# Output projection in fp16 high and low parts: an attention and recurrence kernel with a hand-written order of eight steps

## Chip, cores and metric

The kernel runs on one core of one Trainium2 chip. The metric is the device time of one execution in microseconds (us), taken as the median of the runs.

## The reference

A batch of 32 sequences x (256 positions, 128 features) goes through an attention block and then through a gated recurrence over the batch index:

```python
h = rms_norm(_layernorm(x), norm_weight)            # eps 1e-5 and float32 eps
q, k, v = split(h @ w_qkv.T)                        # 16 heads of 64; rotary embedding on q and k
k, v = concat(persist_mem, k), concat(persist_mem, v)   # 4 more keys and values per head
scores = where(causal, einsum(q, k) * 64**-0.5, min)
out = einsum(softmax(scores), v)                    # 256 x 1024 per sequence
x = x + out @ w_out.T                               # 1024 -> 128: the output projection
xn = _layernorm(x)                                  # scan over the 32 sequences, state c is 256 x 128 here
ft, it = sigmoid(xt @ wf.T + c @ uf.T + bf), sigmoid(xt @ wi.T + c @ ui.T + bi)
gt = tanh(xt @ wc.T + c @ uc.T + bc)
c = ft * c + it * gt                                # after the last step:
x = x + tanh(xn @ wo.T + c_final @ uo.T + bo)
```

All inputs and the output are float32.

## The kernel before

A software pipeline runs over `j`, the number of the sequence that enters. In iteration `j` the kernel projects q and k of sequence `j`, does the softmax and the value product of `j - 1`, normalises and projects out `j - 2` (called `cj`), and takes the recurrence one sequence on with `j - 3` (`dj`). Each iteration has eight steps, `s` = 0 to 7, one per pair of heads. Every engine has a `body(j, p)` that writes out its own instructions step by step, in a fixed order; semaphores tie the engines together. There is no scheduler: what stands ahead in an engine's `body` runs ahead.

What a step holds, and its names: `project` (TensorE, q and k of one pair, three fp16 products of high and low parts), `rotate` (VectorE, the two products of the rotary embedding, which read the projection's bank), `swap` (two DMAs from SyncE's queue that exchange neighbouring rows of `rope_b` into `rope_c`), `rope_add` (GpSimd, `rope_a + rope_c` into `qk`), `hi` (ScalarE, the fp16 copy `qk_h`), `scores_for_max` (TensorE, fp16 scores into `bank_sm`), `maxima` (VectorE), `scores_t` (TensorE, the exact scores of `j - 1` into `bank_st`), `exp` (ScalarE), `prob_add` (GpSimd), `attend` (TensorE, into `bank_pv`), `raw_copy` (ScalarE, `bank_pv` into `raw`). `sums` collects the softmax denominators in `bank_sum`; `transpose_top` turns the maxima, and `copy_top` (ScalarE) copies them back for the next scores.

The output projection of `cj` goes through these functions. `invert` (VectorE, step 1) makes 1/l; `store_linv` and `spread_linv` (SyncE's queue, step 2) bring it to DRAM and from there, repeated over partitions, into `rinv` by four DMAs. `divide` (VectorE) multiplies `raw` by `rinv` in place, quarter by quarter `n` = 0 to 3: 0 and 1 in step 4, 2 and 3 in step 5. `project_out` (TensorE) multiplies a quarter of `raw` by `wo_sb` in float32, two quarters in step 5 and two in step 6, right after `project`. `residual` and `second_stats` (VectorE, step 6), `rstd` (GpSimd, step 7) and `second_norm` (ScalarE, step 7) make the input of the recurrence, `transpose_xn`, `xt_high`, `xt_low`, `gates`, `gate_tanh` and `state` take it on in the next iteration:

```python
if s in (5, 6) and c and j != NB:
    project_out(j - 2, p, 2 * (s - 5))
    project_out(j - 2, p, 2 * (s - 5) + 1)
```

## Time and profile before

| what | value |
|---|---|
| median of 3 runs | 1133.06 us (1131.0 to 1133.95) |
| the profiled execution | 1133.03 us, of which the span from first to last instruction is 1131.2 us |
| TensorE matmul busy | 1080.3 us, 95% of the span |
| VectorE, ScalarE, GpSimd busy | 930.0, 698.4, 634.8 us (82, 62, 56%) |
| mean granted TensorE clock | 0.988 of full speed |

The span is what the trace covers; 1.8 us lie around it. The profiled execution and the median agree within 0.03 us. Busy shares are means over the whole span; in the steady part the pipeline repeats every iteration, so a stretch of one iteration is what to look at.

### The profile page before, as it was taken

The numbers are of one execution on the slowest core, as the hardware profiler recorded it, in microseconds if no ns is written. First come the engines' busy times: TensorE is split into PE (matmuls) and PEld (weight loads), VectorE is DVE, ScalarE is ACT, GpSimd is POOL, SyncE is SP. The second block draws the span as 40 slices with busy tenths as digits, with TensorE's granted clock in tenths as the row PEclk, the third lists the DMA queues.
The fourth block names the chain that finished last, engine by engine and source line by source line (L and its number), as shares of the span: only waits on it lengthen the run. The fifth ranks groups of instructions, "written<-read, shape, count | busy, mean of one in ns | idle before, by whom it ended". The sixth has DMA issues, their size and how long they took to land.

```text
span 1131.2 us, 47261 instructions
## 1 busy us (share of the span) xinstructions
PE 1080.3 (95%) x18443; PEld 813.6 (72%) x18443; DVE 930.0 (82%) x3305; ACT 698.4 (62%) x1575; POOL 634.8 (56%) x816
## 2 busy tenths in 40 slices
PE   3879999999999999999999999999999999999996
PEld 2457777777777776777777777677777777777784
DVE  5778888888888888888888888788888888888745
ACT  3556666666666666666666666666665666666644
POOL 3545665576565647656555665555565565556420
PEclk8889999999999999999999999999999999999999
DMA  6213343332333442233333233333323333332215
GB/s 204 95 62 112 111 115 114 115 95 89 111 111 114 115 114 90 90 111 115 115 115 115 83 100 115 107 114 115 115 78 98 114 115 111 108 112 92 68 36 150
DMA packets 78031, 120.52 MB, mean 107 GB/s; under 512 B 13041, under 2 KB 35954, under 8 KB 77682
## 3 DMA queue, kind: packets, MB, share of 16 engines
q1 hardware_dynamic: 68714, 111.20, 32.5%
q10 hardware_dynamic: 9096, 6.30, 2.1%
q8 instruction: 147, 2.41, 1.0%
q14 instruction: 74, 0.61, 0.2%
HBM read 41.56 MB, written 8.78 MB: 45 GB/s over the span
## 4 chain that ended last, share of the span: by engine, by line
PE 59%; DVE 16%; DMA 14%; SPq 4%; issue 3%; POOL 2%; ACT 1%; DVEq 0%; POOLq 0%
PE bank_pv L1142 11%; PE bank L1034 11%; DMA rope_c<-rope_b 10%; PE bank_st L1098 8%; PE bank_sum L1179 5%; PE bank_sum L1163 4%; DVE masked L809 4%; PE bank_sm L1073 4%; PE bank L1056 3%; DMA linv_scratch<-linv 3%; SPq L312 3%; DVE linv L832 2%; DVE rope_a L798 2%; PE bank L1281 2%; PE bank L1283 2%
## 5 line engine op out<-in xcount | busy, mean ns | idle before, releaser
L407 POOL TENSOR_TENSOR qk<-rope_a,rope_c 128x512 f32<-128x512 f32 x256 | 341.0, 1332 | 312.9 <-DMA rope_c<-rope_b 288.9
L809 DVE CUSTOM_DVE_ANT_0 masked<-bank_sm,mask_q 128x132 bf16<-128x132 f32 (+1 forms) x1024 | 307.1, 355 | 17.7 <-PE bank_sm L1073 17.2
L798 DVE TENSOR_TENSOR rope_a<-bank,cos 128x512 f32<-128x512 f32 x256 | 174.1, 680 | 130.1 <-PE bank L1034 83.7
L400 POOL TENSOR_TENSOR prob<-prob 128x264 f32<-128x264 f32 x256 | 210.8, 823 | 117.1 <-ACT prob L544 108.3
L529 ACT ACTIVATE qk_h<-qk 128x512 f16<-128x512 f32 x256 | 160.4, 627 | 172.2 <-POOL qk L407 171.7
L544 ACT ACTIVATE prob<-bank_st 128x784 f32<-128x784 f32 x256 | 209.3, 817 | 59.7 <-PE bank_st L1107 58.9
L1142 PE MATMUL bank_pv<-prob,v_sb 128*64 128x256 f32 (+1 forms) x2048 | 224.8, 340 | 0.6 <-DVE raw L825 0.6
L1098 PE MATMUL bank_st<-qk 64*64 64x256 f32 (+3 forms) x4096 | 186.3, 299 | 0.4 <-issue 0.2
L1098 PEld LDWEIGHTS bank_st<-qk 64*64 64x64 f32 x4096 | 167.7, 134 | 9.6 <-issue 1.3
L799 DVE TENSOR_TENSOR rope_b<-bank,sin 128x512 f32<-128x512 f32 x256 | 173.8, 679 | 0.0
L1142 PEld LDWEIGHTS bank_pv<-prob,v_sb 128*64 128x64 f32 x2048 | 124.3, 136 | 54.4 <-issue 0.9
L1034 PE MATMUL bank<-h_hi,w_hi 128*128 128x256 f16 x512 | 143.5, 280 | 5.8 <-DVE rope_b L799 5.0
L1034 PE MATMUL bank<-h_hi,w_lo 128*128 128x256 f16 x512 | 141.8, 277 | 0.0
L1034 PE MATMUL bank<-h_lo,w_hi 128*128 128x256 f16 x512 | 141.6, 277 | 0.0
L1179 PE MATMUL bank_sum<-wo_sb,raw 128*128 128x128 f32 x992 | 122.7, 276 | 0.0
L1179 PEld LDWEIGHTS bank_sum<-wo_sb,raw 128*128 128x128 f32 x992 | 116.0, 192 | 1.9 <-DVE raw L845 1.1
L578 ACT ACTIVATE v_sb<-bank 128x512 f32<-128x512 f32 x128 | 75.8, 593 | 48.2 <-PE bank L1053 28.7
L569 ACT ACTIVATE raw<-bank_pv 128x256 f32<-128x256 f32 x256 | 97.7, 382 | 4.1 <-PE bank_pv L1148 3.1
L845 DVE SCALAR_TENSOR_TENSOR raw<-rinv,raw 128x512 f32<-128x512 f32 x124 | 96.6, 819 | 2.0 <-DMA rinv<-linv_scratch 1.8
L1073 PEld LDWEIGHTS bank_sm<-qk_h 64*64 64x64 f16 x2048 | 37.6, 105 | 82.7 <-issue 56.6
L1073 PE MATMUL bank_sm<-qk_h 64*64 64x68 f16 (+3 forms) x2048 | 86.7, 246 | 4.4 <-ACT qk_h L529 3.1
L809 DVE DVE_READ_ACCUMULATOR2_ANT top<- 128x1 bf16 x1024 | 85.7, 84 | 0.1
(237 smaller groups left out, 1732.1 us busy)
## 6 DMA issues: line engine op xcount, KB each, us to landing
rope_c<-rope_b SPq DMA_DIRECT2D x512, 128.0 KB, 2.3
rinv<-linv_scratch SPq DMA_DIRECT2D x124, 256.0 KB, 4.8
out<-x_sb SPq DMA_DIRECT2D x16, 256.0 KB, 3.7
linv_scratch<-linv SPq DMA_DIRECT2D x62, 64.0 KB, 2.1
x_sb<-x ACTq DMA_DIRECT2D x28, 128.0 KB, 5.5
xt<-w_qkv_t ACTq DMA_DIRECT2D x1, 1024.0 KB, 5.3
v_end<-v_end_scratch SPq DMA_DIRECT2D x64, 8.0 KB
v_sb<-pm_v SPq DMA_DIRECT2D x63, 8.0 KB
```

The lines of the kernel that those rows point to most:

```text
L400: G.tensor_tensor(prob_2[:, s % 4, :, :], prob[:, s % 4, :, 0:NT - Q1], prob[:, s % 4, :, C0 + Q1:SCOL], ALU.add).then_inc(S["prob_added"], 1)
L407: G.tensor_tensor(qk[:, s, :].rearrange("p (u n) -> p u n", u=2)[:, :, 0:NT], rope_a[:, (NPAIR * j + s) % 3, :].rearrange("p (u n) -> p u ...
L529: A.activation(qk_h[:, s, :].rearrange("p (u n) -> p u n", u=2)[:, :, 0:NT], qk[:, s, :].rearrange("p (u n) -> p u n", u=2)[:, :, 0:NT], A ...
L544: A.activation(prob[:, s % 4, :, :], ps_st[:, :, 0:SCOL], ACT.Exp).then_inc(S["exp_done"], 1)
L798: V.tensor_tensor(rope_a[:, (NPAIR * j + s) % 3, :], proj_bank(j, s)[:, :], cos[:, :], ALU.mult)
L799: V.tensor_tensor(rope_b[:, s % 2, :], proj_bank(j, s)[:, :], sin[:, :], ALU.mult).then_inc(S["qk_read"], 1)
L809: ins = V.tensor_tensor_reduce(masked[:, e, c0:c0 + n], ps_sm[:, e, c0:c0 + n], mask_q[:, c0:c0 + n], 1.0, LOWEST, ALU.add, ALU.max, top[: ...
L1034: last = T.matmul(proj_bank(j, s)[:, u * NT:(u + 1) * NT], W[q][:, col:col + P], H[p][:, par, NPM:NKEY], start=(i == 0), stop=(i == 2))
L1073: last = T.matmul(ps_sm[OWN[SIDE[qb]], e, c0:c0 + n], qk_h[OWN[e], s, qb * HB:qb * HB + HB], qk_h[OWN[e], s, NT:NT + n], start=True, stop= ...
L1098: T.matmul(ps_st[OWN[SIDE[kb]], e, st_cols(blk)], qk[OWN[e], s, NT + kb * HB:NT + kb * HB + HB], qk[OWN[e], s, q0:NT], start=(kc == 0), st ...
L1142: last = T.matmul(ps_pv[OWN[e], q0:NT], v_sb[:, kc, col:col + DH], prob[:, s % 4, e, c0:c0 + NT - q0], start=(kc == 0), stop=(kc == 1))
L1179: last = T.matmul(y_out(cj)[:, q * D:(q + 1) * D], raw[:, par, s, q * P:(q + 1) * P], wo_sb[:, s, :], start=(alone and s == 0 and q == 0), ...
```

## The change: what it does

- The weights of the output projection are kept as two fp16 tiles, `wo_hi` and `wo_lo` (scaled by 64), made once near the start by one ScalarE and one VectorE instruction.
- After `divide` each quarter of `raw` gets a high part, a fp16 copy (`y_high`, ScalarE, steps 4 and 5), and a low part, the rest (`y_low`, GpSimd, steps 4 and 5). `project_out` makes three fp16 products (high by high, high by low, low by high) where it made one float32 product. Both parts live in `y_hl`, whose memory is also `rinv`.
- `project_out` of quarters 0 and 1 moves to the front of step 6, that of quarters 2 and 3 to the end of step 6. `residual` and `second_stats` move to step 7, `second_norm` to step 0 of the next iteration, with `transpose_xn` and `gates` at the ends of steps 0 to 2, and the other work of the recurrence a step later.
- `spread_linv` issues its four DMAs in two halves, after `swap` of step 2 and of step 3.
- `state` has four parts in place of three: its first two operations stand apart, in steps 2 and 3.
- For the last sequence the low parts are made on VectorE (`y_low_last`).

```diff
         f_lo = sb("f_lo", [P, 8, P], f16)
-        wo_sb = sb("wo_sb", [P, NPAIR, D], f32)
+        wo_hi = sb("wo_hi", [P, NPAIR, D], f16)
+        wo_lo = sb("wo_lo", [P, NPAIR, D], f16)
...
-        rinv = sb("rinv", [P, NPAIR, NT], f32)
+        y_hl = sb("y_hl", [P, 4, 2, 2 * NT], f16)
+        rinv = y_hl[:, :, :, :].rearrange("p n u m -> p (n u m)").bitcast(f32).rearrange("p (s n) -> p s n", s=NPAIR)
...
-            def spread_linv(cj):
+            def spread_linv(cj, half):
...
                 sp.wait_ge(S["linv_stored"], 32 * (cj + 1))
                 sp.sem_inc(S["sp_tick"], 1)
-                wait(sp, S["norm_done"], 4 * cj)
+                wait(sp, S["y_ready"], cj)
                 sp.sem_inc(S["sp_tick"], 1)
-                for half in range(2):
-                    for e in range(2):
-                        src = linv_dram[e:e + 1, 2 * half:2 * half + 2, :, :].rearrange("o k b n -> o (k b n)")
-                        sp.dma_start(rinv[OWN[e], 4 * half:4 * half + 4, :].rearrange("p s n -> p (s n)"),
-                                     src.to_broadcast([64, 4 * NT])).then_inc(spread[half], 16)
+                for e in range(2):
+                    src = linv_dram[e:e + 1, 2 * half:2 * half + 2, :, :].rearrange("o k b n -> o (k b n)")
+                    sp.dma_start(rinv[OWN[e], 4 * half:4 * half + 4, :].rearrange("p s n -> p (s n)"),
+                                 src.to_broadcast([64, 4 * NT])).then_inc(spread[half], 16)
...
-                    if c and s == 2 and j - 2 < NB - 1:
-                        spread_linv(j - 2)
+                    if c and s in (2, 3) and j - 2 < NB - 1:
+                        spread_linv(j - 2, s - 2)
...
+            def y_low(cj, par, n):
+
+                pool.wait_ge(S["y_hi_done"], 4 * cj + n + 1)
+                G.tensor_tensor(y_hl[:, n, 1, :].rearrange("p (s n) -> p s n", s=2), raw[:, par, 2 * n:2 * n + 2, :],
+                                y_hl[:, n, 0, :].rearrange("p (s n) -> p s n", s=2), ALU.subtract).then_inc(S["y_lo_done"], 1)
...
-                    if c and s == 7 and j < NB:
-                        rstd(j - 2)
...
                     if s >= 1 and a:
                         rope_add(j, s - 1)
+                    if s == 4 and c and j < NB:
+                        y_low(j - 2, p, 0)
+                        y_low(j - 2, p, 1)
+                    if s == 7 and c and j < NB:
+                        rstd(j - 2)
                     if b:
                         prob_add(j - 1, s)
+                    if s == 5 and c and j < NB:
+                        y_low(j - 2, p, 2)
+                        y_low(j - 2, p, 3)
+                    if s in (5, 6) and j == NB:
+                        y_low(j - 2, p, 2 * (s - 5))
+                        y_low(j - 2, p, 2 * (s - 5) + 1)
...
+            def y_high(cj, par, n):
+
+                act.wait_ge(S["norm_done"], 4 * cj + n + 1)
+                A.activation(y_hl[:, n, 0, :].rearrange("p (s n) -> p s n", s=2), raw[:, par, 2 * n:2 * n + 2, :],
+                             ACT.Copy).then_inc(S["y_hi_done"], 1)
...
-                    if s == 3 and b:
-                        copy_top(j - 1, 1)
...
-                    if s == 0 and d and j != NB + 1:
+                    if s == (0 if j > NB else 1) and d and j != NB + 1:
                         xt_high(j - 3)
...
                         gate_tanh_last(j - 3)
-                    elif s in (1, 2) and d and j - 3 < NB - 1:
-                        gate_tanh(j - 3, s - 1)
+                    elif s in (2, 3) and d and j - 3 < NB - 1:
+                        gate_tanh(j - 3, s - 2)
+                    if s == 3 and b:
+                        copy_top(j - 1, 1)
...
-                    if s == 7 and c and j < NB:
-                        second_norm(j - 2)
+                    if s == 0 and d and j <= NB:
+                        second_norm(j - 3)
...
                     if s >= 1 and b:
                         raw_copy(j - 1, 1 - p, s - 1)
+                    if s in (4, 5) and c and j <= NB:
+                        y_high(j - 2, p, 2 * (s - 4))
+                        y_high(j - 2, p, 2 * (s - 4) + 1)
...
+                V.scalar_tensor_tensor(wo_lo[:, :, :].rearrange("p c d -> p (c d)"), o_raw, WS,
+                                       wo_hi[:, :, :].rearrange("p c d -> p (c d)"), ALU.mult,
+                                       ALU.subtract).then_inc(S["casts_dve"], 1)
...
+            def y_low_last(cj, par, n):
+
+                dve.wait_ge(S["y_hi_done"], 4 * cj + n + 1)
+                V.tensor_tensor(y_hl[:, n, 1, :].rearrange("p (s n) -> p s n", s=2), raw[:, par, 2 * n:2 * n + 2, :],
+                                y_hl[:, n, 0, :].rearrange("p (s n) -> p s n", s=2), ALU.subtract).then_inc(S["y_lo_done"], 1)
...
                 dve.wait_ge(S["y_ready"], cj + 1)
-                V.tensor_tensor(at3(x_sb, cj), y_out(cj), at3(x_sb, cj), ALU.add).then_inc(S["x1_done"], 1)
+                V.scalar_tensor_tensor(at3(x_sb, cj), y_out(cj), 1.0 / WS, at3(x_sb, cj), ALU.mult,
+                                       ALU.add).then_inc(S["x1_done"], 1)
...
-                        dve.wait_ge(S["gate_read"], 2 * dj + 2)
+                        dve.wait_ge(S["gate_read"], 2 * dj + 1)
+                    wait(dve, S["dve_s"], 3 * dj)
                     V.scalar_tensor_tensor(ga[:, :], th[:, 0, :], 1.0, c2[:, :], ALU.add, ALU.mult).then_inc(S["dve_s"], 1)
-                    if dj == NB - 1:
-                        dve.wait_ge(S["gate_read"], 2 * dj + 2)
+                elif part == 1:
+                    dve.wait_ge(S["gate_read"], 2 * dj + 2)
                     V.scalar_tensor_tensor(gb[:, :], th[:, 1, :], 1.0, th[:, 2, :], ALU.add, ALU.mult).then_inc(S["dve_s"], 1)
-                elif part == 1:
+                elif part == 2:
                     dve.wait_ge(S["dve_s"], 3 * dj + 2)
                     V.scalar_tensor_tensor(c2[:, :], ga[:, :], 0.5, gb[:, :], ALU.mult, ALU.add).then_inc(S["dve_s"], 1)
...
+                    if s == 7 and c and j < NB:
+                        residual(j - 2)
+                    if s == 1 and c:
+                        end_add(j - 2, p)
                     if a:
                         rotate(j, s)
-                    if s == 1 and c:
-                        end_add(j - 2, p)
-                    if s == 0 and d and j != NB + 1:
+                    if s == (0 if j > NB else 1) and d and j != NB + 1:
                         xt_low(j - 3)
...
+                    if s == 2 and d and j != NB + 1:
+                        state(j - 3, 0)
                     if s == 3 and d and j != NB + 1:
-                        state(j - 3, 0)
+                        state(j - 3, 1)
+                        state(j - 3, 2)
...
                     if s == 4 and c and j - 2 < NB - 1:
                         divide(j - 2, p, 0)
                         divide(j - 2, p, 1)
-                    if s == 4 and d and j != NB + 1:
-                        state(j - 3, 1)
...
+                    if s == (6 if j >= NB else 7) and c:
                         second_stats(j - 2)
...
                     if s == 6 and d and j < NB:
-                        state(j - 3, 2)
+                        state(j - 3, 3)
...
-                pe.wait_ge(S["norm_done"], 4 * cj + n + 1)
+                pe.wait_ge(S["y_lo_done"], 4 * cj + n + 1)
+                if cj == 0 and n == 0:
+                    pe.wait_ge(S["casts_dve"], 7)
                 alone = cj >= NB - 2
                 for s in (2 * n, 2 * n + 1):
                     for q in range(QT):
-                        last = T.matmul(y_out(cj)[:, q * D:(q + 1) * D], raw[:, par, s, q * P:(q + 1) * P], wo_sb[:, s, :],
-                                        start=(alone and s == 0 and q == 0), stop=(s == NPAIR - 1 and q == QT - 1),
-                                        skip_group_check=True)
+                        at = s % 2 * NT + q * P
+                        for i, (u, v) in enumerate(SPLIT):
+                            last = T.matmul(y_out(cj)[:, q * D:(q + 1) * D], y_hl[:, n, u, at:at + P], WO[v][:, s, :],
+                                            start=(alone and s == 0 and q == 0 and i == 0),
+                                            stop=(s == NPAIR - 1 and q == QT - 1 and i == 2), skip_group_check=True)
                 if n == 3:
                     last.then_inc(S["y_ready"], 1)
...
-                    elif s == 0 and d and j <= NB:
-                        transpose_xn(j, j - 3)
-                    if s in (1, 2) and d and j <= NB:
-                        gates(j, j - 3, s - 1)
...
-                    if s in (5, 6) and c and j != NB:
+                    if s == 6 and c and j < NB:
+                        project_out(j - 2, p, 0)
+                        project_out(j - 2, p, 1)
...
+                    if s == 6 and c and j < NB:
+                        project_out(j - 2, p, 2)
+                        project_out(j - 2, p, 3)
                     if s in (2, 4, 7) and b:
                         sums(j - 1, (2, 4, 7).index(s))
-                if isinstance(j, int) and j == 2:
-                    pe.wait_ge(S["casts_dve"], 6)
+                    if s == 0 and d and j <= NB:
+                        transpose_xn(j, j - 3)
+                    if s in (1, 2) and d and j <= NB:
+                        gates(j, j - 3, s - 1)
```

In these listings a row is an instruction with its source line, operation, output<-inputs and shape; "x2" stands for two in a row. GpSimd, steps 4 and 5 of an iteration with all stages active, before:

```order
L407 TENSOR_TENSOR qk<-rope_a,rope_c 128x2x256
L400 TENSOR_TENSOR prob<-prob 128x264
L407 TENSOR_TENSOR qk<-rope_a,rope_c 128x2x256
L400 TENSOR_TENSOR prob<-prob 128x264
L407 TENSOR_TENSOR qk<-rope_a,rope_c 128x2x256
```

and now (L408 is `rope_add`, L401 `prob_add`, L416 `y_low`):

```order
L408 TENSOR_TENSOR qk<-rope_a,rope_c 128x2x256
L416 TENSOR_TENSOR y_hl<-raw,y_hl 128x512 x2
L401 TENSOR_TENSOR prob<-prob 128x264
L408 TENSOR_TENSOR qk<-rope_a,rope_c 128x2x256
L401 TENSOR_TENSOR prob<-prob 128x264
L416 TENSOR_TENSOR y_hl<-raw,y_hl 128x512 x2
L408 TENSOR_TENSOR qk<-rope_a,rope_c 128x2x256
```

Between the first `rope_add` of the listing and the last, four instructions over 128x512 were put, two ahead of the `prob_add` of step 4 and two behind that of step 5.

ScalarE, steps 4 and 5, now (L597 `value_copy`, L563 `exp`, L588 `raw_copy`, L655 `y_high`, L548 `hi`, L496 `h_high`); before, the two rows of L655 were not there and the rest stood in the same order:

```order
L597 ACTIVATE v_sb<-bank 128x512
L561 ACTIVATE prob_end<-bank_st 16x2x16
L563 ACTIVATE prob<-bank_st 128x784
L588 ACTIVATE raw<-bank_pv 128x256
L655 ACTIVATE y_hl<-raw 128x512 x2
L548 ACTIVATE qk_h<-qk 128x2x256
L496 ACTIVATE h_hi<-bank,nw 128x256
L563 ACTIVATE prob<-bank_st 128x784
L588 ACTIVATE raw<-bank_pv 128x256
L655 ACTIVATE y_hl<-raw 128x512 x2
L548 ACTIVATE qk_h<-qk 128x2x256
```

The high parts stand ahead of the fp16 copy of q and k (`hi`) of the same step.

TensorE, end of step 6 now, between the last `attend` (L1191) and `transpose_top` of step 7 (L1131), the first rows of the 24 small fp16 products of quarters 2 and 3:

```order
L1191 MATMUL bank_pv<-prob,v_sb 64x132 x2
L1232 MATMUL bank_sum<-wo_hi,y_hl 128x128
L1232 MATMUL bank_sum<-wo_lo,y_hl 128x128
L1232 MATMUL bank_sum<-wo_hi,y_hl 128x128 x2
L1232 MATMUL bank_sum<-wo_lo,y_hl 128x128
```

and before, where step 6 passed from `attend` straight to `transpose_top`, and its float32 block stood behind `project`:

```order
L1034 MATMUL bank<-h_lo,w_hi 128x256
L1179 MATMUL bank_sum<-wo_sb,raw 128x128 x8
L1053 MATMUL bank<-w_hi,h_hi 128x512
```

A block of 8 float32 products became 24 fp16 products, and the second block of an iteration moved behind the rest of step 6.

## Rows read from the trace of the kernel before

**Rows 1.** The page: busy time and share of each engine

```profile
PE 1080.3 (95%) x18443; PEld 813.6 (72%) x18443; DVE 930.0 (82%) x3305; ACT 698.4 (62%) x1575; POOL 634.8 (56%) x816
```

**Rows 2.** Windows of one iteration: PE, PEld, DVE, ACT, POOL busy, clock, DMA share, GB/s

```profile
500.00:532.40 32.40, 32.37 (x572) 24.60 (x568) 27.73 (x103) 21.07 (x49) 19.79 (x25) 1.00 0.36 109
```

**Rows 3.** Timeline, residual of sequences 1 and 29: start, duration

```profile
132.79 0.41 DVE L850 TENSOR_TENSOR x_sb<-bank_sum,x_sb 128x256 f32<-128x256 f32 x1
...
1056.48 0.41 DVE L850 TENSOR_TENSOR x_sb<-bank_sum,x_sb 128x256 f32<-128x256 f32 x1
```

**Rows 4.** Waits: waiting engine <- what it waited for: us in total, times, longest

```profile
POOL qk L407 <- DMA rope_c<-rope_b: 288.9, 128, 8.3
...
PE bank_sm L1081 <- DVE top L809: 13.1, 20, 4.3
...
PE bank L1034 <- DVE rope_b L799: 5.0, 7, 1.5
```

**Rows 5.** TensorE's timeline, steps 4 to 7 of one iteration: start, duration

```profile
516.50 0.28 PE L1034 MATMUL bank<-h_hi,w_hi 128*128 128x256 f16 x1
...
520.57 0.28 PE L1034 MATMUL bank<-h_hi,w_hi 128*128 128x256 f16 x1
...
521.45 1.95 PE L1179 MATMUL bank_sum<-wo_sb,raw 128*128 128x128 f32 x16
523.33 0.34 PE L1073 MATMUL bank_sm<-qk_h 64*64 64x68 f16 x8
...
525.16 0.28 PE L1034 MATMUL bank<-h_hi,w_hi 128*128 128x256 f16 x1
...
525.83 1.95 PE L1179 MATMUL bank_sum<-wo_sb,raw 128*128 128x128 f32 x16
527.62 0.38 PE L1053 MATMUL bank<-w_hi,h_hi 128*128 128x512 f16 x1
...
528.36 0.34 PE L1073 MATMUL bank_sm<-qk_h 64*64 64x68 f16 x8
...
530.18 0.28 PE L1081 MATMUL bank_sm<-ident_b,top 128*128 128x128 bf16 x2
```

**Rows 6.** TensorE's timeline near the end: first and last of 12 fp16 products

```profile
1089.62 0.22 PE L1241 MATMUL bank_pv<-f_hi,xt 128*128 128x128 f16 x1
...
1090.24 0.22 PE L1241 MATMUL bank_pv<-f_hi,xt 128*128 128x128 f16 x1
```

**Rows 7.** Groups by form: the weight loads of those products: busy, mean ns

```profile
L1241 PEld LDWEIGHTS bank<-f_hi,xt 128*128 128x128 f16 x40 | 3.3, 98 | 0.5
```

**Rows 8.** SyncE's queue, steps 2 and 3: issue start, duration

```profile
513.70 2.40 SPq L312 DMA_DIRECT2D rinv<-linv_scratch  x4
516.28 2.19 SPq L294 DMA_DIRECT2D rope_c<-rope_b  x2
```

**Rows 9.** VectorE's timeline: divide of quarters 0, 1 (step 4) and 2, 3 (step 5)

```profile
519.91 1.29 DVE L845 SCALAR_TENSOR_TENSOR raw<-rinv,raw 128x512 f32<-128x512 f32 x2
...
523.98 1.84 DVE L845 SCALAR_TENSOR_TENSOR raw<-rinv,raw 128x512 f32<-128x512 f32 x2
```

**Rows 10.** ScalarE's timeline: raw_copy of step 4, hi of step 5

```profile
520.23 0.38 ACT L569 ACTIVATE raw<-bank_pv 128x256 f32<-128x256 f32 x1
...
526.97 0.63 ACT L529 ACTIVATE qk_h<-qk 128x512 f16<-128x512 f32 x1 [0.90 <-POOL qk L407]
```

**Rows 11.** GpSimd's timeline, steps 4 to 6

```profile
522.78 1.27 POOL L407 TENSOR_TENSOR qk<-rope_a,rope_c 128x512 f32<-128x512 f32 x1 [4.95 <-DMA rope_c<-rope_b]
524.02 1.25 POOL L400 TENSOR_TENSOR prob<-prob 128x264 f32<-128x264 f32 x1
525.23 1.71 POOL L407 TENSOR_TENSOR qk<-rope_a,rope_c 128x512 f32<-128x512 f32 x1
526.90 0.75 POOL L400 TENSOR_TENSOR prob<-prob 128x264 f32<-128x264 f32 x1
527.61 1.28 POOL L407 TENSOR_TENSOR qk<-rope_a,rope_c 128x512 f32<-128x512 f32 x1
```

32 lines of the change are left out of this document (21 added, 11 removed).

## The prediction, written before the changed kernel had run

> **What bounds the kernel now.** I read the busy shares first. TensorE's matmuls fill 95% of the span, VectorE 82%, ScalarE 62%, GpSimd 56% [rows 1]. Then one iteration from the steady part: in 32.40 us TensorE is busy for 32.37 at full clock (1.00), GpSimd for 19.79, ScalarE for 21.07, VectorE for 27.73 [rows 2]. So inside an undisturbed iteration only TensorE's own work counts. The mean iteration is a little longer: from the residual of sequence 1 to that of sequence 29 there are 28 iterations in 923.7 us, 32.99 us each [rows 3], 0.6 more than the undisturbed one. Some of that is in the waits: TensorE waited 20 times, 13.1 us in total, for the maxima ahead of `transpose_top` (one wait of 4.3 us is in the drain at the end), and 7 times, 5.0 us, for `rotate` [rows 4]. The long waits of GpSimd for the swap DMAs (288.9 us, [rows 4]) mostly cost nothing, since TensorE goes on meanwhile. Time can be won by taking work off TensorE, and lost by making something late that TensorE needs.
>
> **TensorE's work.** The float32 block of step 6 starts at 525.83 and the next instruction at 527.62: 1.79 us for 8 products (16 records, two each) [rows 5]. No fp16 block of the projection exists in this trace, but the same shape does: 12 fp16 products of 128x128 by 128 columns, each with its own weight load, start from 1089.62 to 1090.24, 11 distances of 0.056 us [rows 6]. So 24 products take 1.35 us. Two blocks per sequence: 2 x (1.79 - 1.35) = 0.88 us, times 32 sequences = **-28.2 us**. The waits need no new price here. The recurrence's matmuls only change place.
>
> The Trainium skill, page "TensorE: Matmul & The Clock Gate", section "Back-to-back issue gap", gives a sustained pace of about 81 ns for a product of 128 columns with its weight load and about 56 ns only for the isolated one. By that rule a block would take 24 x 0.081 = 1.94 us, more than the float32 block, and the change would have no gain at all on TensorE. Rows 6 are loads and products in alternation and show 56 ns, so I go by them.
>
> **What the halved spread removes.** The four DMAs of 1/l are issued from 513.70 for 2.40 us, and the swap of step 3 only behind them, at 516.28 [rows 8]. It landed so late that `rope_add` of step 4 had GpSimd idle for 4.95 us and began at 522.78 [rows 11]. With only half of the spread ahead the swap goes out some 1.2 us sooner and has half the bytes before it, so I expect that `rope_add` near 519, before the low parts begin. Where the delay reached TensorE it is in its waits for `rotate`. Moving `gates` behind `attend` also starts VectorE's step 1 work earlier, so that the maxima of step 2 are ready some 0.3 us before `transpose_top` asks. The waits that could go are 13.1 - 4.3 + 5.0 = 13.8 us at most [rows 4], some of them at the start; I take **-8 us** (bounds 0 and -13.8).
>
> **What the new chain adds.** I follow one iteration on a clock that starts with TensorE's step 4, at 516.50 [rows 5]. When does TensorE ask for quarter 3? Step 4 lasts 4.07 us (516.50 to 520.57). Step 5 was 4.59 (to 525.16), without its block 2.80. Step 6 was 5.02 (to 530.18), without its block 3.23; with quarters 0 and 1 in front, 4.58. Quarter 2 then takes 0.67. TensorE reaches quarter 3 at 4.07 + 2.80 + 4.58 + 0.67 = 12.12 [rows 5].
>
> When is its low part ready? The divides of step 4 start at 3.41 (519.91), the first is done at about 4.05 [rows 9]; `raw_copy` ends at 4.11 (520.23 + 0.38) [rows 10]. A high part is a ScalarE copy of 128x512 float32 to fp16, as `hi` is, 0.63 us [rows 10]: done at 4.7, so the first low part starts at 4.75. A low part has no row. The nearest is `rope_add`, also a two-input GpSimd operation over 128x512: 1.27 to 1.28 us uncontended, start to start 1.24 [rows 11]. GpSimd then has, in order, two low parts (2.48), `prob_add` of step 4 (0.71 start to start, 526.90 to 527.61), `rope_add` (1.24), `prob_add` of step 5 (0.71), and two more low parts (1.24 + 1.28) [rows 11]. That is 7.66 us, done at 12.41: 0.3 us late if nothing disturbs it.
>
> But something does. The divides of step 5 took 1.84 us for two instead of 1.29 [rows 9], and GpSimd, working beside them, took 1.25 instead of 0.75 for `prob_add` and 1.71 instead of 1.28 for `rope_add` [rows 11]: a VectorE operation with two inputs in SBUF and a GpSimd one hinder each other, at 0.93 us for GpSimd per pair of divides. The divides of quarters 2 and 3 now start at about 4.07 + 0.87 + 1.2 = 6.1, while GpSimd is in its second low part. So the last low part ends at 13.34, with the semaphore 13.4: 1.28 us behind TensorE. The low part of the state on VectorE, late in step 6, has two SBUF inputs as well and falls on low part 2 or 3; in the proportion of the divides (0.93 per 1.29) its 0.4 us cost up to 0.3 more. I take a stall of 1.45 us at quarter 3, in the 30 iterations from 2 to 31: **+43.5 us**. Bounds: the low part at nothing, where the stall is 0, and at the contended 1.71 us each, which adds 4 x 0.43 = 1.7 to make 3.2.
>
> Who waits behind the low parts? `rope_add` of step 6, behind it `hi` on ScalarE (0.63), and behind that `copy_top` (0.5), which the scores of step 7 need. `rope_add` ends at 14.7, `hi` at 15.3, the copy at about 15.9. TensorE, itself delayed, asks at about 13.5 + 0.67 + 0.13 + 0.74 + 0.80 = 15.8. A tie; I put 0.1 x 30 = **+3 us**. Quarters 0 and 1 are asked for at 4.07 + 2.80 + 0.67 = 7.5 and 8.2 and are ready at 6.0 and 7.8 even contended. ScalarE's four copies (2.5 us per iteration on an engine that is idle for 11, [rows 2]) hide. `residual` waits for the end of step 6, but `rotate` behind it needs a later projection anyway. `second_stats` now ends in step 7, `rstd` and `second_norm` about 2.7 us into the next iteration, where `transpose_xn` asks at 3.4: hidden with 0.6 to spare, and if that went it would cost what it exceeds.
>
> Start and end: the two weight casts (about 1 us each) fall in iteration 1, where TensorE isn't full, and at the end the shorter products of the last sequence win back about as much: 0, give or take 1.5.
>
> Sum, against the profiled execution's 1133.0 us (the median of the runs is the same): 1133.0 - 28.2 - 8 + 43.5 + 3 = **1143 us**.
>
> **The rivals.** (A) The forecast, a stall of 1.3 to 1.9 us per iteration: 39 to 57 us for -36.2 won and +3, so 1139 to 1157. Chance 0.45.
> (B) The low parts hide: the collision with the divides isn't repeated, or low parts are somewhat quicker. With a stall of 0.3 us (9 us) and the tie it is 1133 - 36.2 + 12 = 1109, range 1099 to 1118. For it speaks that the uncontended chain and TensorE differ by only 0.3 us, against it the rows of the one place where both engines met. It decides below a stall of (36.2 - 3) / 30 = 1.1 us. Chance 0.22.
> (C) Half of the collision: stall 0.7 to 1.0, 1121 to 1130, chance 0.10; stall 1.0 to 1.2, no change, chance 0.12.
> (D) GpSimd is slower with fp16 in and out, 1.71 us: stall 3.2 us, +96 in place of 43.5: 1195; half of that 1168. No row has a fp16 operand on GpSimd. Chance 0.07.
> (E) Weight loads set the pace. A load takes 98 ns [rows 7]; if the loads of `y_hl` don't overlap, a block is 24 x 0.098 = 2.35 us, and TensorE pays 2 x (2.35 - 1.79) x 32 = +36 instead of -28, while it meets quarter 3 later by 1.5 us, so that the stall is gone: 1133 + 36 - 8 + 3 = 1164. Against it speaks the 56 ns pitch [rows 6]. Chance 0.04. By the pace in the Trainium skill, same page and section, it would be +10 us of work, a stall of about 0.55 us and 1154.
>
> **How the numbers follow.** The likeliest case gives 1143, its own range 1139 to 1157. The range must reach into (B), whose middle is 1109, and to the lower half of (D): 1109 to 1167. A measurement of this kernel can tell about 0.3%, 3.4 us, from no change. Faster: 0.22 + 0.10 = 0.32; same: 0.12; slower: 0.45 + 0.07 + 0.04 = 0.56.
>
> **What would show it.** TensorE's block should be 24 products in 1.35 us. The waits should name TensorE's projection line with the low parts on GpSimd as releaser, some 30 times and 1.3 to 1.9 us each, at quarter 3 and not at 0 or 1. GpSimd's low part should take 1.28 us alone and near 1.7 beside the divides; its busy time should rise by about 30 x 5.1 = 155 us. `rope_add` of step 4 should start at about 2.5 us after step 4 and not at 6.3. The waits for the maxima should shrink. The prediction is wrong if the low parts are much shorter than 1.28 us, if the divides and the low parts don't meet, or if the moved recurrence makes TensorE wait at the ends of steps 0 to 2, where the margins are 0.1 to 0.6 us.

## The result and the profile after

The changed kernel takes **1166.66 us** (median of 4 runs, 1165.62 to 1167.87) against 1132.03 for the kernel before beside it: ratio 1.0304, 95% interval 1.0282 to 1.0327. It is slower by 34.6 us. The prediction had the direction and a change of +10. The two profiled executions, from which the rows come, differ by 32.6 us (1133.0 and 1165.6).

The page of the changed kernel, busy time of each engine, to be held against [rows 1]:

```profile
PE 1068.8 (92%) x18955; PEld 785.1 (67%) x18955; DVE 994.2 (85%) x3310; ACT 763.5 (66%) x1704; POOL 773.3 (66%) x940
```

TensorE has less to do than before and a smaller share of a longer span: it waits. GpSimd gained 138.5 us (155 were forecast). VectorE gained 64.2 us, although only five VectorE operations were added (x3305 to x3310), one near the start and four for the last sequence. That is the first sign of what the prediction missed.

Where in the program the time is lost is read from an instruction that stands at the same place in both, the reciprocal of 1/l (`invert`). VectorE's timeline of the kernel before, sequences 0 and 29 (start, duration):

```profile
80.30 1.75 DVE L832 RECIPROCAL linv<-bank_sum 128x256 f32<-128x256 f32 x1
...
1037.35 1.75 DVE L832 RECIPROCAL linv<-bank_sum 128x256 f32<-128x256 f32 x1
```

and of the changed one:

```profile
81.89 1.75 DVE L866 RECIPROCAL linv<-bank_sum 128x256 f32<-128x256 f32 x1
...
1066.30 1.75 DVE L866 RECIPROCAL linv<-bank_sum 128x256 f32<-128x256 f32 x1
```

The start costs 1.6 us. The 29 iterations between take 957.05 us before (33.00 each) and 984.41 after (33.95 each), 27.4 more. The rest of the growth of the span (1131.2 to 1163.8), 3.6 us, lies behind sequence 29. So it is a loss of 0.94 us per iteration in the mean.

TensorE's waits in the changed kernel (waiting engine, what it waited for: us in total, times, longest), against [rows 4]:

```profile
PE bank_sum L1232 <- POOL y_hl L416: 11.9, 46, 0.7
PE bank_sm L1123 <- DVE top L843: 11.7, 30, 0.4
...
PE bank L1103 <- DVE h_lo L773: 9.1, 10, 1.2
PE bank_sm L1123 <- ACT top_t L578: 8.8, 29, 1.2
PE bank_sm L1131 <- DVE top L843: 8.1, 3, 5.3
PE bank_pv L1191 <- DMA v_sb<-pm_v: 5.6, 13, 1.2
PE bank L1084 <- DVE rope_b L833: 3.0, 10, 0.5
```

Before there were two such rows of size; now there are seven. The low parts (L416) are only one of them, 46 waits of at most 0.7 us, not 30 of 1.45. The others are the maxima ahead of `scores_for_max` (L1123), the low part of h, `copy_top` (`top_t`, 29 times), the maxima ahead of `transpose_top` (L1131, 3 times), the persistent values' DMA and `rotate`.

One iteration shows them. TensorE's timeline of the changed kernel, the five rows with a wait between 503 and 514, and the borders of the blocks of quarter 2 (509.34 to 509.96) and quarter 3 (510.46 to 511.08):

```profile
503.47 0.28 PE L1084 MATMUL bank<-h_hi,w_hi 128*128 128x256 f16 x1 [0.17 <-DVE rope_b L833]
...
505.14 0.23 PE L1232 MATMUL bank_sum<-wo_hi,y_hl 128*128 128x128 f16 x1 [0.17 <-POOL y_hl L416]
...
507.29 0.34 PE L1123 MATMUL bank_sm<-qk_h 64*64 64x68 f16 x8 [0.39 <-DVE top L843]
...
509.34 0.23 PE L1232 MATMUL bank_sum<-wo_hi,y_hl 128*128 128x128 f16 x1
...
509.96 0.22 PE L1232 MATMUL bank_sum<-wo_hi,y_hl 128*128 128x128 f16 x1
510.46 0.23 PE L1232 MATMUL bank_sum<-wo_hi,y_hl 128*128 128x128 f16 x1 [0.28 <-POOL y_hl L416]
...
511.08 0.22 PE L1232 MATMUL bank_sum<-wo_hi,y_hl 128*128 128x128 f16 x1
511.14 0.27 PE L1131 MATMUL bank_sm<-ident_b,top 128*128 128x128 bf16 x2
...
513.11 0.34 PE L1123 MATMUL bank_sm<-qk_h 64*64 64x68 f16 x8 [0.27 <-ACT top_t L578]
```

The 12 products of a quarter start in 0.62 us, the pace of 0.056 us that [rows 6] had promised. VectorE's timeline of the same iteration, the state's `c` (L946), the two pairs of divides (L879) and `c_lo` (L949):

```profile
496.76 0.89 DVE L946 SCALAR_TENSOR_TENSOR c<-ga,gb 128x256 f32<-128x256 f32 x1
...
499.89 2.33 DVE L879 SCALAR_TENSOR_TENSOR raw<-y_hl,raw 128x512 f32<-128x512 f32 x2
...
503.34 2.29 DVE L879 SCALAR_TENSOR_TENSOR raw<-y_hl,raw 128x512 f32<-128x512 f32 x2
...
509.58 1.10 DVE L949 SCALAR_TENSOR_TENSOR c_lo<-c,c_hi 128x256 f16<-128x256 f32 x1
```

and GpSimd's:

```profile
496.62 0.75 POOL L401 TENSOR_TENSOR prob<-prob 128x264 f32<-128x264 f32 x1 [0.64 <-ACT prob L563]
499.79 1.27 POOL L408 TENSOR_TENSOR qk<-rope_a,rope_c 128x512 f32<-128x512 f32 x1 [2.43 <-DMA rope_c<-rope_b]
502.36 2.73 POOL L416 TENSOR_TENSOR y_hl<-raw,y_hl 128x512 f16<-128x512 f32 x2 [1.29 <-ACT y_hl L655]
505.04 1.19 POOL L401 TENSOR_TENSOR prob<-prob 128x264 f32<-128x264 f32 x1
...
508.12 2.28 POOL L416 TENSOR_TENSOR y_hl<-raw,y_hl 128x512 f16<-128x512 f32 x2
```

Each of VectorE's four begins while a GpSimd operation runs or meets one, and ends late by about what that one still had to go. In the second pair both engines lose: the two low parts beside it take 2.73 us, the two at 508.12 only 2.28. `rope_add` ends at 501.06; a pair of divides takes 1.29 [rows 9] and would end at 502.35, and the row ends at 502.22. The second low part ends at 510.40; `c_lo` with its 0.42 behind it would end at 510.82, and the row ends at 510.68. Over the whole run such operations are longer too (min/median/max in ns); how much of that comes with the low parts is seen only in the experiments. Before:

```profile
L845 DVE SCALAR_TENSOR_TENSOR raw<-rinv,raw x124: 676/683/1246, 90.9 to 1080.9; 128x512 f32<-128x512 f32 x124
...
L907 DVE SCALAR_TENSOR_TENSOR c_lo<-c,c_hi x32: 408/422/482, 135.2 to 1110.8; 128x256 f16<-128x256 f32 x32
```

After, with the low part itself:

```profile
L879 DVE SCALAR_TENSOR_TENSOR raw<-y_hl,raw x124: 676/1216/1801, 92.5 to 1111.9; 128x512 f32<-128x512 f32 x124
L416 POOL TENSOR_TENSOR y_hl<-raw,y_hl x124: 1149/1164/1692, 95.8 to 1117.4; 128x512 f16<-128x512 f32 x124
...
L949 DVE SCALAR_TENSOR_TENSOR c_lo<-c,c_hi x32: 404/1102/1117, 137.7 to 1143.4; 128x256 f16<-128x256 f32 x32
```

The Trainium skill, page "SBUF — State Buffer", section "SBUF: two separate sides", says that VectorE with two SBUF inputs and GpSimd share one pair of ports, and that whoever starts first holds it for its whole instruction while the other blocks. The rows above agree to within 0.14 us.

### The profile page after: what moved, and what is told of

The parts are those of the page before. It is cut to its first block, busy times and chain, and to the rows that moved or that the text cites. A ratio compares the mean times of both kernels' runs of the same rounds, so it can differ in the third digit from the quotient of the medians.

```text
span 1163.8 us, 48636 instructions
## 1 busy us (share of the span) xinstructions
PE 1068.8 (92%) x18955; PEld 785.1 (67%) x18955; DVE 994.2 (85%) x3310; ACT 763.5 (66%) x1704; POOL 773.3 (66%) x940
## 4 chain that ended last, share of the span: by engine, by line
PE 37%; POOL 18%; DVE 15%; issue 13%; DMA 8%; ACT 6%; SPq 1%; POOLq 0%; ACTq 0%; DVEq 0%
POOL qk L408 8%; PE bank_pv L1191 7%; PE bank L1084 7%; DMA rope_c<-rope_b 7%; POOL y_hl L416 6%; PE bank_st L1147 5%; POOL prob L401 4%; DVE masked L843 4%; PE bank_sum L1212 4%; PE bank_sm L1123 3%; DVE rope_a L832 3%; PE bank L1334 3%; DVE raw L879 2%; PE bank L1336 2%; DVE rope_b L833 2%
## 5 line engine op out<-in xcount | busy, mean ns | idle before, releaser
L408 POOL TENSOR_TENSOR qk<-rope_a,rope_c 128x512 f32<-128x512 f32 x256 | 339.3, 1326 | 210.6 <-DMA rope_c<-rope_b 201.0
L563 ACT ACTIVATE prob<-bank_st 128x784 f32<-128x784 f32 x256 | 209.7, 819 | 95.9 <-PE bank_st L1156 95.0
L548 ACT ACTIVATE qk_h<-qk 128x512 f16<-128x512 f32 x256 | 160.3, 626 | 121.6 <-POOL qk L408 120.0
L401 POOL TENSOR_TENSOR prob<-prob 128x264 f32<-128x264 f32 x256 | 209.6, 819 | 39.0 <-ACT prob L563 38.7
L1191 PE MATMUL bank_pv<-prob,v_sb 128*64 128x256 f32 (+1 forms) x2048 | 224.7, 340 | 5.8 <-DMA v_sb<-pm_v 5.6
L416 POOL TENSOR_TENSOR y_hl<-raw,y_hl 128x512 f16<-128x512 f32 x124 | 153.5, 1260 | 21.9 <-ACT y_hl L655 21.9
L1191 PEld LDWEIGHTS bank_pv<-prob,v_sb 128*64 128x64 f32 x2048 | 125.6, 136 | 59.2 <-issue 7.8
L879 DVE SCALAR_TENSOR_TENSOR raw<-y_hl,raw 128x512 f32<-128x512 f32 x124 | 135.3, 1130 | 5.3 <-DMA y_hl<-linv_scratch 5.0
L1232 PE MATMUL bank_sum<-wo_hi,y_hl 128*128 128x128 f16 x992 | 100.0, 220 | 13.4 <-POOL y_hl L416 11.9
L1123 PEld LDWEIGHTS bank_sm<-qk_h 64*64 64x64 f16 x2048 | 39.1, 105 | 106.8 <-issue 70.8
L655 ACT ACTIVATE y_hl<-raw 128x512 f16<-128x512 f32 x128 | 79.9, 631 | 47.5 <-DVE raw L879 45.6
L1123 PE MATMUL bank_sm<-qk_h 64*64 64x68 f16 (+3 forms) x2048 | 86.8, 246 | 23.2 <-DVE top L843 11.7
L588 ACT ACTIVATE raw<-bank_pv 128x256 f32<-128x256 f32 x256 | 97.4, 380 | 2.9 <-PE bank_pv L1197 2.5
L1232 PEld LDWEIGHTS bank_sum<-wo_hi,y_hl 128*128 128x128 f16 x992 | 78.6, 98 | 27.5 <-POOL y_hl L416 25.4
```

Source lines behind the costliest of these rows:

```text
L401: G.tensor_tensor(prob_2[:, s % 4, :, :], prob[:, s % 4, :, 0:NT - Q1], prob[:, s % 4, :, C0 + Q1:SCOL], ALU.add).then_inc(S["prob_added"], 1)
L408: G.tensor_tensor(qk[:, s, :].rearrange("p (u n) -> p u n", u=2)[:, :, 0:NT], rope_a[:, (NPAIR * j + s) % 3, :].rearrange("p (u n) -> p u ...
L416: G.tensor_tensor(y_hl[:, n, 1, :].rearrange("p (s n) -> p s n", s=2), raw[:, par, 2 * n:2 * n + 2, :], y_hl[:, n, 0, :].rearrange("p (s n ...
L563: A.activation(prob[:, s % 4, :, :], ps_st[:, :, 0:SCOL], ACT.Exp).then_inc(S["exp_done"], 1)
L1123: last = T.matmul(ps_sm[OWN[SIDE[qb]], e, c0:c0 + n], qk_h[OWN[e], s, qb * HB:qb * HB + HB], qk_h[OWN[e], s, NT:NT + n], start=True, stop= ...
L1191: last = T.matmul(ps_pv[OWN[e], q0:NT], v_sb[:, kc, col:col + DH], prob[:, s % 4, e, c0:c0 + NT - q0], start=(kc == 0), stop=(kc == 1))
```

## The experiments

All ratios are to the kernel before, run on the same chip; brackets are 95% intervals. Besides the ratio I give the mean iteration, from the starts of the reciprocals of sequences 0 and 29.

**1. No low parts.** For all but the last two sequences the low parts are not made; the third product reads the high part again, so TensorE does as much.

```diff
-                    if s == 4 and c and j < NB:
-                        y_low(j - 2, p, 0)
-                        y_low(j - 2, p, 1)
...
-                            last = T.matmul(y_out(cj)[:, q * D:(q + 1) * D], y_hl[:, n, u, at:at + P], WO[v][:, s, :],
+                            last = T.matmul(y_out(cj)[:, q * D:(q + 1) * D], y_hl[:, n, u if low else 0, at:at + P], WO[v][:, s, :],
```

> The changed kernel without the low parts of sequences 0 to 29 (the products that read them read the high part instead, so TensorE has the same 24 products per block; the low parts' share of the result is left out). Theory A (the low parts on GpSimd and their collisions with VectorE make the loss): the 0.88 us of TensorE's work per iteration and the removed waits come through, 32.2 us or less per iteration, 1103 to 1112 us. Rival B (the moved order, the high parts and the later residual chain cost by themselves): stays above the kernel before, 1135 to 1155 us. GpSimd is the engine whose busy time falls, by about 150 us.

Measured: 1127.93 us, 0.9964 [0.9939, 0.9989], iteration 32.55, between the two theories. Its ten runs spread from 1122.69 to 1132.55, and the profiled one is the fastest of them, so its iteration is some 0.1 to 0.2 us short of the typical one. The low parts cost 38.7 us in all. Without them the change would have been a small gain, not the large one that its shorter products promise: something else costs too.

**2. The low parts on VectorE**, in steps 5 and 6 behind `rotate`.

```diff
+                    if s in (5, 6) and c and j < NB:
+                        y_low_last(j - 2, p, 2 * (s - 5))
+                        y_low_last(j - 2, p, 2 * (s - 5) + 1)
```

> All low parts on VectorE, two in step 5 and two in step 6, each pair behind rotate. Theory A: the low parts take about 0.65 us each there, the divides fall back to 0.64 to 0.7 us each from 1.13, and 1120 to 1135 us result. Rival C (it is only that one more link stands in the chain from divide to product, on whichever engine): 1155 us or more. A third outcome, VectorE itself too full (30 of 32 us), would show as TensorE waiting for rotate and maxima and give 1135 to 1150.

Measured: 1216.12 us, 1.0750 [1.0703, 1.0796]. TensorE's longest row of waits there:

```profile
PE bank L1100 <- DVE h_lo L767: 50.4, 28, 2.4
```

This is above what I had named for theory A and for a full VectorE. Rival C, one more link in the chain on whichever engine, allows it, but TensorE's longest wait is for `h_low` and not for the low parts (11.5 us, 18 times), so the run doesn't test the length of the chain. VectorE, not full by its share (1073.9 of 1218.2 us), has no room in steps 5 and 6: what is put there arrives at TensorE. And the divides did not fall back, although GpSimd makes low parts for only one sequence, near the end:

```profile
L873 DVE SCALAR_TENSOR_TENSOR raw<-y_hl,raw 128x512 f32<-128x512 f32 x124 | 137.4, 1147 | 1.0 <-DMA y_hl<-linv_scratch 0.9
```

Their mean of 1.147 us (1.130 in the changed kernel, 0.819 before) comes from meeting `rope_add` and `prob_add`.

**3. Divides that read one input** (`raw` times 1.0 in place of 1/l, so that the output isn't normalised).

```diff
-                V.scalar_tensor_tensor(o, rinv[:, 2 * n:2 * n + 2, :], 1.0, o, ALU.mult, ALU.mult).then_inc(S["norm_done"], 1)
+                V.tensor_scalar(o, o, 1.0, None, ALU.mult).then_inc(S["norm_done"], 1)
```

> The divides of sequences 0 to 30 are replaced by a multiplication of the same tile by 1.0, with one SBUF input instead of two (the division by l is left out); the low parts stay on GpSimd. Theory A, collisions of two two-input operations: divides without the 1.13 us mean, GpSimd's low part at 1.27, last low part 0.9 to 2 us earlier, 1118 to 1138 us. Rival C, the length of the chain without collisions: 1155 us or more. If a one-input operation collides as well, its duration will show it.

Measured: 1141.11 us, 1.0080 [1.0053, 1.0108]; 25.6 us less than the changed kernel. It is no clean test, as the one-input operation is shorter by itself (0.41 us) and collides as well:

```profile
L879 DVE TENSOR_SCALAR raw<-raw x124: 410/735/1523, 94.0 to 1086.7; 128x512 f32<-128x512 f32 x124
```

Its mean is 0.803 us, 0.33 below that of the real divide; four per iteration come to 1.3 us of VectorE's time, and 0.87 us of it reach TensorE (iteration 33.08 in place of 33.95). So the time of VectorE in steps 4 and 5 is on the path. Whether it gets there through VectorE's next operations or through the low parts behind the divides, the run doesn't separate: TensorE's waits for the low parts fell as well, from 11.9 us to 5.5. (That the one-input form collides too fits the same section of the Trainium skill, which has it for operations in the two-port mode; no run here shows which mode it ran in.)

**4. The moved order in float32.** The changed kernel's order and halved spread, with `wo_sb` in float32 and no high or low parts (its `project_out` waits for the divides).

```diff
-                pe.wait_ge(S["y_lo_done"], 4 * cj + n + 1)
+                pe.wait_ge(S["norm_done"], 4 * cj + n + 1)
...
-                            last = T.matmul(y_out(cj)[:, q * D:(q + 1) * D], y_hl[:, n, u, at:at + P], WO[v][:, s, :],
+                        last = T.matmul(y_out(cj)[:, q * D:(q + 1) * D], raw[:, par, s, q * P:(q + 1) * P], wo_sb[:, s, :],
```

> The changed kernel's order, its halved spread, its split state and moved recurrence, but the projection in float32 as before, with no high or low parts. Theory A: the order costs nothing and removes the waits for the maxima and for rotate: 1120 to 1130 us. Rival B: the order costs, 1138 to 1150 us.

Measured: 1150.41 us, 1.0171 [1.0142, 1.0201], iteration 33.43, at the upper end of rival B. So the order alone costs 18 us, which the prediction had at nothing. From here to experiment 1, which adds the fp16 products, the high parts and the weight casts, it is -22.5 us between the medians, about 0.7 per iteration, and 0.88 us between the profiled iterations. The second is the 2 x 0.44 of the forecast, but it rests on the fastest run of experiment 1. VectorE is busy for 970.0 us here: 40 of the 64.2 us that it gained in the changed kernel come without any low part. Its divides and `c_lo`:

```profile
L857 DVE SCALAR_TENSOR_TENSOR raw<-y_hl,raw 128x512 f32<-128x512 f32 x124 | 120.0, 1007 | 6.5 <-DMA y_hl<-linv_scratch 6.3
L926 DVE SCALAR_TENSOR_TENSOR c_lo<-c,c_hi x32: 409/848/861, 133.1 to 1126.7; 128x256 f16<-128x256 f32 x32
```

TensorE's timeline of this kernel in steps 5 and 6 shows where it waits:

```profile
492.18 0.88 PE L1164 MATMUL bank_pv<-prob,v_sb 128*64 128x256 f32 x8 [0.67 <-DMA v_sb<-pm_v]
493.73 0.28 PE L1057 MATMUL bank<-h_hi,w_hi 128*128 128x256 f16 x1 [0.67 <-DVE rope_b L811]
...
497.61 0.34 PE L1096 MATMUL bank_sm<-qk_h 64*64 64x68 f16 x8 [0.39 <-DVE top L821]
```

Step 5 has lost its block of 1.8 us of products, step 6 has its second block at the end, and TensorE comes early: to `attend` of step 5, where it waits for the persistent values' DMA, and to `project` and the scores of step 6, where it waits for VectorE.

**5. The halved spread alone**, in the kernel before.

```diff
-                    if c and s == 2 and j - 2 < NB - 1:
-                        spread_linv(j - 2)
+                    if c and s in (2, 3) and j - 2 < NB - 1:
+                        spread_linv(j - 2, s - 2)
```

> The kernel before with the spread of 1/l issued in halves, one behind the swap of step 2 and one behind the swap of step 3, and nothing else. In the order-only kernel TensorE had new waits: for v_sb's persistent rows (a small DMA that stands behind the second half on SyncE's queue) and for rotate and maxima (the divides of step 4 now meet rope_add). Theory D (the halved spread makes both): 1134 to 1142 us, divides above the 0.82 us mean, waits for v_sb. Theory E (the halves only remove waits, the order's loss is in the moved recurrence and blocks): 1122 to 1130 us.

Measured: 1134.12 us, 1.0026 [1.0007, 1.0044], at the lower end of theory D. No gain. The earlier swap brings `rope_add` of step 4 into the divides: their mean is 0.968 us here and 0.819 before.

**6. Whole spread in the moved order** (experiment 4, all four DMAs in step 2).

```diff
-                    if c and s in (2, 3) and j - 2 < NB - 1:
-                        spread_linv(j - 2, s - 2)
+                    if c and s == 2 and j - 2 < NB - 1:
+                        spread_linv(j - 2, 0)
+                        spread_linv(j - 2, 1)
```

> The order-only kernel with float32 projection, but all four DMAs of the spread issued in step 2 again. Theory D: the waits for v_sb and the slow divides go, 1130 to 1140 us, less than the 1150 with halves. Theory E: 1148 or more, since the moved work remains and the swap of step 3 is late again. The drain of the last two sequences (about 4 us of the loss) should remain in both.

Measured: 1154.74 us, 1.0193 [1.0151, 1.0235]; its profiled run took 1161.3. Not better than experiment 4, so the halved spread isn't what the order costs. Nor are longer divides needed for the loss: here they are nearly as short as before (0.819), and TensorE's longest row of waits is for `rotate`:

```profile
L858 DVE SCALAR_TENSOR_TENSOR raw<-y_hl,raw 128x512 f32<-128x512 f32 x124 | 98.3, 832 | 1.1 <-DMA y_hl<-linv_scratch 1.1
...
PE bank L1058 <- DVE rope_b L812: 20.9, 28, 2.2
```

**7. Low parts of quarters 0 and 1 only.** For the other two the third product reads the high part again, as in experiment 1.

```diff
-                    if s == 5 and c and j < NB:
-                        y_low(j - 2, p, 2)
-                        y_low(j - 2, p, 3)
```

> The changed kernel with the low parts of quarters 0 and 1 alone on GpSimd; for quarters 2 and 3 of sequences 0 to 29 the products read the high part twice (those low parts are left out). None gave 1128, four give 1167. If the loss goes by the number of low parts: 1145 to 1150. If only the last of the chain counts (quarter 3 behind rope_add and two prob_add): 1128 to 1138. If the first two are the ones that hurt, by meeting the divides and pushing the rest: 1150 or more.

Measured: 1141.67 us, 1.0100 [1.0074, 1.0127], iteration 33.15. None, two and four low parts give 1127.9, 1141.7 and 1166.7: 6.9 us for each of the first two, 12.5 for each of the others. None of my three outcomes fits; the loss doesn't go by the number.

**8. Divides and high parts of quarters 0 and 1 earlier**, in step 4 ahead of `maxima(1)` and `raw_copy`.

```diff
+                    if s == 4 and c and j < NB:
+                        divide(j - 2, p, 0)
+                        divide(j - 2, p, 1)
                     if s == 5 and c and j - 2 < NB - 1:
                         divide(j - 2, p, 2)
...
+                    if s == 4 and c and j < NB:
+                        y_high(j - 2, p, 0)
+                        y_high(j - 2, p, 1)
                     if s >= 1 and b:
                         raw_copy(j - 1, 1 - p, s - 1)
```

> The changed kernel, with the divides of quarters 0 and 1 ahead of the maxima of step 4 and their high parts ahead of raw_copy, so that the low parts start 1.3 to 2 us sooner. If the wait at the end of a long chain (divide, high, low, product) is the cost: 1145 to 1155. If it is VectorE's lateness by collisions: about the same as the changed kernel, 1160 to 1170, as the maxima are later by the divides.

Measured: 1154.46 us, 1.0207 [1.0189, 1.0224]. It wins 12 us, and pays in another place. The longest row of TensorE's waits, and that for the low parts:

```profile
PE bank_sm L1129 <- DVE top L846: 28.0, 50, 1.6
...
PE bank_sum L1238 <- POOL y_hl L416: 2.0, 7, 0.4
```

By what I had put down this outcome speaks for the long chain (divide, high part, low part, product) and against collisions as the cost. But the divides are shorter here too (mean 1.042 us for 1.130), so the run doesn't separate the two.

**9. The persistent values' DMA ahead of the second half of the spread**, in the changed kernel.

```diff
+                    if b and s == 3 and c and j < NB:
+                        tails(j - 1, 1)
                     if c and s in (2, 3) and j - 2 < NB - 1:
                         spread_linv(j - 2, s - 2)
```

> The changed kernel, with the DMA of the persistent values (tails, half 1) issued in step 3 ahead of the second half of the spread and not behind it. Theory Q (TensorE's attend in step 5 waits for this row because two broadcasts stand in front of it in SyncE's queue): the waits of TensorE for v_sb (5.6 us, 13 times, and the unseen part, about 0.2 us per iteration) go, 1160 to 1163 us, ratio to the kernel before 1.025 to 1.028. Rival (the queue time only moves: the second half of 1/l and the swap of step 3 are issued 0.6 us later, so the divides 0 and 1 or rope_add of step 4 come later): no gain, 1165 to 1169.

Measured: 1162.84 us, 1.0278 [1.0254, 1.0302]. The wait for `v_sb` is gone from the list, and the next ones have grown:

```profile
PE bank L1105 <- DVE h_lo L775: 12.8, 16, 1.2
...
PE bank L1086 <- DVE rope_b L835: 6.5, 18, 0.8
```

The difference of 3 us to the changed kernel is about the reach of the two intervals; I read it as a small gain, not shown beyond doubt.

**10. Both edits of 8 and 9** (the diff is those two together).

> The changed kernel with the divides of quarters 0 and 1 ahead of the maxima of step 4, the high parts of these ahead of raw_copy, and the tails' DMA ahead of the second half of the spread. If both waits are separate, the gains add: x7 gave 1154.5, less 4 us is 1150, ratio 1.017. If the wait for v_sb was already slack behind a later wait in the same iteration, it stays at 1154, ratio 1.0207.

Measured: 1155.17 us, 1.0210 [1.0186, 1.0233]: the gains don't add. The likely reason is that the wait for `v_sb` stood in front of one for VectorE that ends at about the same time.

**11. Only the recurrence moved**, in the kernel before: its rows of the change's diff alone, among them

```diff
-                    elif s == 0 and d and j <= NB:
-                        transpose_xn(j, j - 3)
-                    if s in (1, 2) and d and j <= NB:
-                        gates(j, j - 3, s - 1)
...
+                    if s == 0 and d and j <= NB:
+                        transpose_xn(j, j - 3)
+                    if s in (1, 2) and d and j <= NB:
+                        gates(j, j - 3, s - 1)
```

> The kernel before (float32 projection in steps 5 and 6, whole spread, residual and statistics in step 6), with only the recurrence moved as in the change: the transposes and gates at the ends of steps 0 to 2, the other operations of the recurrence a step later, the state in four parts, second_norm in step 0. Theory R (moving the recurrence is what costs in the moved order): about 1145 us or more, ratio 1.010 to 1.018, most of the 18 us that the whole moved order costs. Theory P (the cost is in the projection's blocks in step 6 and the residual in step 7; the recurrence is free): 1131 to 1135, ratio within 0.3% of 1. In between, 1136 to 1144, both have a share, R's being the excess over 1133.

Measured: 1140.58 us, 1.0076 [1.0055, 1.0097]: between the two theories, with one new wait in each iteration:

```profile
PE bank_pv L1145 <- DVE raw L825: 16.5, 30, 0.6
```

This is `end_add` on VectorE in step 1, which the change puts ahead of `rotate` and my kernel had left behind it. So the next run takes that too.

**12. The recurrence moved, and `end_add` ahead of `rotate`.**

```diff
+                    if s == 1 and c:
+                        end_add(j - 2, p)
                     if a:
                         rotate(j, s)
-                    if s == 1 and c:
-                        end_add(j - 2, p)
```

> The kernel x10 (before with only the recurrence moved) with end_add also ahead of rotate in step 1, as the change has it. x10 had a new wait of 0.6 us per iteration in step 1, TensorE's attend for the end values' addition on VectorE. If that wait is all that the moved recurrence costs, it goes and the time is at or below the kernel before: 1122 to 1132, ratio 0.992 to 1.001. If the recurrence costs by itself, it stays above 1136.

Measured: **1124.69 us, 0.9938 [0.9921, 0.9956]**, iteration 32.67. The recurrence's part of the moved order is no loss but a gain of 7 us, and this kernel, in float32 throughout the projection, is faster than both. Its waits for the maxima and for `rotate`:

```profile
PE bank_sm L1084 <- DVE top L809: 10.3, 10, 4.3
...
PE bank L1037 <- DVE rope_b L799: 2.1, 4, 1.1
```

against 20 and 7 times in [rows 4]. And it has the long `c`, with no low part anywhere:

```profile
L905 DVE SCALAR_TENSOR_TENSOR c<-ga,gb x32: 424/882/967, 120.1 to 1101.4; 128x256 f32<-128x256 f32 x32
```

In its new place `c` meets `prob_add`; before it took 0.416 us in the median and in the changed kernel 0.886.

**13. Experiment 4 with the first block back in step 5.**

```diff
-                    if s == 6 and c and j < NB:
+                    if s == 5 and c and j < NB:
                         project_out(j - 2, p, 0)
                         project_out(j - 2, p, 1)
```

> The moved order in float32 with the halved spread (x4, 1150.4 us), but the products of quarters 0 and 1 back in step 5 as in the kernel before. Theory C (cover): the block of 1.8 us in step 5 covered TensorE while VectorE did the divides; without it TensorE comes to attend of step 5, project of step 6 and the scores of step 6 too early. Then the waits in steps 5 and 6 (about 0.9 us per iteration in x4, 0.5 in before) fall by 0.4 and the time is 1132 to 1140, ratio 1.000 to 1.007. Rival (the block at the end of step 6 and the residual in step 7 cost): it stays at 1146 to 1152.

Measured: 1141.33 us, 1.0089 [1.0061, 1.0117], iteration 33.21, just above the range that I had given the cover theory. Of the 25.7 us between experiments 12 and 4, 9.1 are gone, and TensorE's waits for `rotate` fell with them, in experiment 4 and here:

```profile
PE bank L1057 <- DVE rope_b L811: 8.5, 16, 1.0
...
PE bank L1057 <- DVE rope_b L811: 1.9, 4, 0.8
```

The other 16.6 us stay, with the second block at the end of step 6, the residual and statistics in step 7 and the halved spread.

To see all of it at once I took, for 26 iterations of the steady part, the distance from each of TensorE's blocks to the next, and summed the shortest ones. The sum is 32.4 to 32.5 us in the four float32 kernels and 31.5 in experiment 1, which also stands for the two below it; what the mean iteration has above it is waiting. Each row is from one profiled execution.

| kernel | iteration | waiting | where most of it is (us per iteration) |
|---|---|---|---|
| before | 33.00 | 0.6 | project 6: 0.14; transpose_top behind step 6: 0.25 |
| 12, recurrence moved | 32.67 | 0.3 | end of step 6: 0.15 |
| 13, + second block moved | 33.21 | 0.7 | quarters 0, 1: 0.20; project 6: 0.14; scores 6: 0.25 |
| 4, + first block moved | 33.43 | 1.0 | attend in 5: 0.18; project 6: 0.26; blocks and scores 6: 0.39 |
| 1, + fp16 and high parts | 32.55 | 1.0 | the same places |
| 7, + two low parts | 33.15 | 1.6 | attend in 5: 0.44; around quarters 0, 1: 0.54; scores 6: 0.42 |
| changed kernel | 33.95 | 2.4 | around quarters 0, 1: 0.71; quarters 2, 3: 0.46; scores 6: 0.46; copy_top: 0.34; attend in 5: 0.20 |

Of the 1.4 us by which the changed kernel's iteration is longer than that of experiment 1, 0.66 stand at the low parts themselves (0.20 ahead of quarter 1, 0.46 at quarters 2 and 3) and 0.34 ahead of the scores that need `copy_top`. VectorE's lateness has 0.54: 0.28 more behind quarter 1, where the next projection waits for `h_low`, and 0.26 more ahead of the scores of step 6. Elsewhere it waits a little less.

## Why the prediction was off

The measured steps are: from before to experiment 12 -7.4 us, to 13 +16.6, to 4 +9.1, to 1 -22.5, to 7 +13.7, to the changed kernel +25.0. They are differences of neighbouring medians, so that they add up to the whole (+34.5 for +34.6) proves nothing; each is good to about 3 us. Against the terms of the prediction:

- **TensorE -28.2: right in mechanism and nearly in size.** Blocks run at 0.056 us per product, as forecast; from experiment 4 to 1 the medians give -22.5, in which the weight casts took back about 1 us at the start (80.07 to 81.03 for the first reciprocal). The pace of 81 ns that the Trainium skill gives ("TensorE: Matmul & The Clock Gate", "Back-to-back issue gap") doesn't hold for these blocks.
- **Halved spread and earlier maxima -8: half wrong.** The halved spread gives +2 alone (experiment 5). In the iteration shown `rope_add` of step 4 starts at 499.79, 3.4 us after step 4 and not 2.5. The moved recurrence gives -7.4, about what I had put down for both.
- **"The recurrence's matmuls only change place", the blocks too: the first step that failed.** I priced the new place of the projection by its operands alone: are the low parts there? The sum 4.07 + 2.80 + 4.58 + 0.67 simply took the block out of step 5, as if TensorE met nobody on the way. But the float32 block in step 5, and the one early in step 6, were also time in which VectorE did its divides, and the queue its transfers, while TensorE needed nothing of them. Moving both away costs 25.7 us (experiments 12, 13, 4), where 0 stood. That it is the lost cover is shown for the first block (9.1 us) by putting it back; in the other 16.6 us block, residual, statistics and spread moved together. The halved spread alone costs 2 us in the kernel before (experiment 5); which of the rest costs was not separated.
- **The stall at quarter 3, +43.5: the second that failed.** The low parts do cost 38.7 us (experiment 1 to the changed kernel), close to the term of 43.5 and 3, but in other places. On the prediction's clock, from TensorE's step 4 on (medians of 26 iterations), the last low part is done at 13.97 us, later than the 13.4 forecast, although one alone takes 1.16 us and not 1.28. And TensorE comes to quarter 2 at about 13.0 in place of 11.45 and to quarter 3 at about 13.7 in place of 12.12, since it has lost time on the way. So quarters 2 and 3 wait for 0.46 us per iteration, not 1.45. I had claimed that quarters 0 and 1 come in time, by 7.8 at the latest; the low part of quarter 1 is done at 8.6, and TensorE waits for it too.
- **The price of a collision.** I took it from rows where GpSimd had paid most and charged GpSimd alone. VectorE pays as well: each divide is 0.31 us longer in the mean (0.819 to 1.130). But not all of this comes with the low parts. Experiment 4 has 1.007 and experiment 1 has 0.943, so the low parts add 0.19 per divide, some 0.75 us over four, in front of `rotate`, `h_low` and the maxima of step 6; `c_lo` grows by 0.25 in the median (0.85 to 1.10), and `c` not at all (0.88 in experiment 12). Experiment 2 has divides of 1.147 with no low part on GpSimd. That the longer divides make VectorE's 0.54 us of lateness is likely and not shown: the longer chain and the collisions were not separated (experiments 3 and 8).
- **`copy_top` +3: right in kind, too small.** 29 waits, 8.8 us.
- **Start and end at nothing:** +1.6 and +3.6 us.

So the forecast of +10 lacked 24.6. The terms account for it so: the order of the blocks 25.7 where 0 stood; the products 5.7 short; the low parts 38.7 where 46.5 stood; the rest within 1 us (-7.4 for -8). 25.7 + 5.7 - 7.8 + 0.6 = 24.2. The 7.8 us too many for the low parts hid a part of what was missing. That 1166.66 lies within the stated 1109 to 1167 is luck: the upper end had been drawn out for the lower half of (D), which didn't happen. Rival (B), that the low parts hide, is refuted by the 38.7 us of experiment 1. The short stall at quarter 3 of (B) and (C) came true, and their times did not. (D) is refuted, since fp16 operands made GpSimd's operation shorter, and (E) by the blocks' pace.

## What to carry to other kernels

In this kernel a block of long, independent work on the bound engine was also cover for what the other engines did meanwhile. So before you move such a block, list which engine catches up under it, and price the move by who is asked earlier. Price a collision of VectorE and GpSimd by who starts first, for both engines, and follow the one that loses to its next consumers; an engine at 82% in the mean can have no room at all in the steps that matter. And test a bundle by its parts: one part of this slower change, applied alone, is a faster kernel.

## What was unexpected in the hardware

- The two-input divide on VectorE has a median of 1.216 us in the changed kernel where it had 0.683, and `c_lo` 1.102 where it had 0.422. In the rows of one iteration the loser waits for the end of the other's instruction and then takes its usual time, to within 0.14 us. It isn't only heavy work on GpSimd that does this: beside `rope_add` and `prob_add` alone the divides of experiment 2 have a mean of 1.147 us.
- The one-input VectorE operation over the same tile also suffers, 0.410 us at best and 0.735 in the median.
- GpSimd subtracts 128x512 with fp16 in one input and the output in 1.149 to 1.164 us, less than the 1.27 of the float32 addition [rows 11]; whether the operation or the types make the difference is open.
